# A graph network's bf16 splits: casts moved from VectorE and GpSimd to ScalarE, and the graph layers' output rows in two halves of PSUM

## The reference, cut to what matters

```python
# mean layers (run twice):  MEAN1, MEAN2
mean = segment_sum(h[src], dst) / max(count, 1);  out = mean @ W_l + b_l + h @ W_r
# graph convolutions (three): GCN1, GCN2, GCN3
h = x @ W
out = segment_sum(h[src] * dis[src] * dis[dst], dst) + h * dis**2 + b
# around each layer: x = layernorm(x + layer(x))
```

## Time and profile before

| what | value |
|---|---|
| median of 3 runs | 8144.81 us (8144.05 to 8150.12) |
| profiled execution, its own time | 8149.13 us |
| its span in the profile | 8147.2 us |
| busy shares | PE 52%, DVE 62%, ACT 35%, POOL 59% |

### The profile page before, as it was taken

The page is one execution under the profiler, slowest core; times in us unless marked ns, Lnnn a source line. Parts: engine busy times, 40 slices in busy tenths (PEclk is TensorE's granted clock), DMA queues, the critical chain, the costliest instruction groups (busy, mean ns, idle before and its releaser), DMA issues.

```text
span 8147.2 us, 70764 instructions
## 1 busy us (share of the span) xinstructions
PE 4234.8 (52%) x19184; PEld 2471.1 (30%) x19184; DVE 5020.9 (62%) x9411; ACT 2884.7 (35%) x5375; POOL 4827.2 (59%) x5030
## 2 busy tenths in 40 slices
PE   2110000000255555666665566566566598999999
PEld 1000000000131111111113111111111398999999
DVE  4654444444568888888786778878887774222232
ACT  0222222222255555555553555555555300010000
POOL 6777777777637777777776777777777500000000
PEclk6555555555565555555555555555555599999999
DMA  5333333333224444444443444444444275766767
GB/s 132 88 98 85 85 87 87 85 85 85 66 86 131 130 131 133 132 131 133 133 131 101 133 131 131 133 133 131 131 133 132 84 268 199 267 223 220 267 228 248
DMA packets 642166, 1129.68 MB, mean 139 GB/s; under 512 B 164844, under 2 KB 422271, under 8 KB 641618
## 3 DMA queue, kind: packets, MB, share of 16 engines
q1 hardware_dynamic: 360112, 437.17, 17.2%
q0 software_dynamic: 159184, 251.10, 14.8%
q10 hardware_dynamic: 122578, 438.40, 13.6%
HBM read 713.46 MB, written 412.70 MB: 138 GB/s over the span
## 4 chain that ended last, share of the span: by engine, by line
POOL 48%; PE 21%; issue 17%; DVE 10%; DMA 4%; ACT 1%; DVEq 0%; POOLq 0%; SPq 0%; ACTq 0%
POOL CG L460 46%; PE psX L736 6%; PE psB L736 6%; PE psA L736 6%; DMA CG<-table,BUF 3%; DVE BUF L1550 2%; PE psO L679 1%; DVE XTQ L1576 1%; DVE BUF L1545 1%; DVE STG L1576 1%; DVE BUF L1542 1%; DVE XTQ L1569 1%; DVE STG L1569 1%; ACT X L1045 1%; POOL EG L519 1%
## 5 line engine op out<-in xcount | busy, mean ns | idle before, releaser
L460 POOL DMA_INDIRECT CG<-table,BUF x4704 | 4482.0, 953 | 1567.5 <-issue 1351.7
L706 PE MATMUL psO<-WE,BUF 128*128 128x384 f32 x1568 | 1141.7, 883 | 381.7 <-DMA BUF<-in_edge_attr 381.7
L1001 ACT ACTIVATE BUF<-iota,EG 128x128 bf16<-128x128 f16 x3136 | 958.0, 387 | 205.1 <-ACT CG L981 103.0
L779 PE MATMUL psA<-ident,F 128*100 128x128 f32 x1 | 0.5, 455 | 1704.3 <-DVEq L1451 1704.3
L486 POOL CAST CG<-EG x35 | 26.9, 769 | 1296.1 <-DVEq L1217 1296.1
L977 ACT COPY psX<-BUF 128x384 f32<-128x384 f32 x392 | 189.0, 482 | 1540.0 <-DVE XTQ L1576 771.0
L706 PEld LDWEIGHTS psO<-WE,BUF 128*128 128x128 f32 x1568 | 459.6, 323 | 893.8 <-DMA BUF<-in_edge_attr 646.5
L1542 DVE TENSOR_SCALAR BUF<-iota,EG 128x392 bf16<-128x392 f16 x1568 | 562.1, 358 | 46.9 <-DMA EG<-step_rows 19.1
L1480 DVE TENSOR_TENSOR terms<-CG,ARENA 128x64 f32<-128x64 f32 x98 | 26.3, 269 | 904.2 <-DMA CG<-table,BUF 903.7
L1545 DVE TENSOR_SCALAR BUF<-iota,EG 128x392 bf16<-128x392 f16 x1568 | 543.4, 347 | 6.5 <-PE psB L716 3.3
L779 PEld LDWEIGHTS psA<-ident,F 128*100 128x100 f32 x1 | 0.2, 162 | 1704.7 <-DVEq L1451 1704.7
(11 more groups left out here) (284 smaller groups left out, 7533.6 us busy)
## 6 DMA issues: line engine op xcount, KB each, us to landing
BUF<-counts SPq DMA_DIRECT2D x245, 784.0 KB, 5.8
BUF<-counts ACTq DMA_DIRECT2D x245, 784.0 KB, 6.4
counts<-BUF SPq DMA_DIRECT2D x1572, 98.0 KB, 2.3
hist<-CG ACTq DMA_DIRECT2D x392, 384.0 KB, 2.4
hist<-CG ACTq DMA_DIRECT2D x196, 416.0 KB, 2.5
CG<-table,BUF POOLq DMA_INDIRECT x4704, 2.5
BUF<-in_edge_attr SPq DMA_DIRECT2D x392, 128.0 KB, 3.3
table<-TB SPq DMA_DIRECT2D x14, 336.0 KB, 2.6
```

Of the source, the lines that this page charges most:

```text
L460: pool.indirect_dma_start(out=rows_in[:, u % RING, k, :], out_offset=None, in_=tab, in_offset=bass.IndirectOffsetOnAxis(ap=SRC[:, u * S + ...
L706: mm = pe.matmul(ETERM[:, s, a, 0:4 * DIM], EA[:, s, a, :], WE[:, m, :, :].rearrange("k c d -> k (c d)"), start=True, stop=True)
L1001: far = nc.scalar.activation(FAR[:, j, a, :], iota16[:, 0:P], ACT.Square, bias=STEP[:, 2 + a, u * CS + j:u * CS + j + 1], scale=-1.0)
```

## The change

It touches only the node rows of MEAN2, GCN1, GCN2 and GCN3 (`SPLIT_HERE`); MEAN1 stays as it was. There:

- ACT casts both parts (new functions `first_part` and `second_part`); DVE does both subtractions (`rest_of_first`, `third_part`), the third part of group g-1 between the table of group g and the rest of group g. GpSimd's loops over these four phases go; only its loop for MEAN1 stays.
- In the three graph phases the product of group g goes to half g % 2 of psO, and PE waits for the table of group g-2 instead of g-1.
- In code order on ACT, the last casts stand behind the last copy of XT (or R) and ahead of the loading loop.

```diff
@@ PE, multiply_group
-                pe.wait_ge(out_used, g + (base + 1))
+                narrow = f in (GCN1, GCN2, GCN3)
+                pe.wait_ge(out_used, base + (max(g, 1) if narrow else g + 1))
@@ ACT, node_phase
                 rows_transposed(f, g)
                 if g and f in (MAX1, MAX2, MEAN1, MEAN2):
                     root_rows(f, g - 1)
+                if g and f in SPLIT_HERE:
+                    if g >= 2:
+                        second_part(f, g - 2)
+                    first_part(f, g - 1)
             if f in (MAX1, MAX2, MEAN1, MEAN2):
                 root_rows(f, NG - 1)
+            if f in SPLIT_HERE:
+                second_part(f, NG - 2)
+                first_part(f, NG - 1)
+                second_part(f, NG - 1)
+
+        def first_part(f, g):
+            act.wait_ge(table_made, PASS_OF_PHASE[f] * NG + g + 1)
+            nc.scalar.copy(PARTS[:, here, 0:DIM], TBW[:, here, :]).then_inc(first_made, 1)
+
+        def second_part(f, g):
+            act.wait_ge(rest_made, (PASS_OF_PHASE[f] - GATHER_PASSES) * NG + g + 1)
+            nc.scalar.copy(PARTS[:, here, DIM:2 * DIM], EGW[:, here, :]).then_inc(second_made, 1)
@@ DVE, take_rows
-                split(here, g)
+                if f in SPLIT_HERE:
+                    if g:
+                        third_part(f, g - 1)
+                    rest_of_first(f, g)
+                else:
+                    split(here, g)
+
+        def rest_of_first(f, g):
+            dve.wait_ge(first_made, SPLIT_HERE.index(f) * NG + g + 1)
+            link(tt(EGW[:, here, :], TBW[:, here, :], PARTS[:, here, 0:DIM], ALU.subtract))
+            dve.sem_inc(rest_made, 1)
+
+        def third_part(f, g):
+            dve.wait_ge(second_made, (PASS_OF_PHASE[f] - GATHER_PASSES) * NG + g + 1)
+            tt(PARTS[:, here, 2 * DIM:3 * DIM], EGW[:, here, :], PARTS[:, here, DIM:2 * DIM],
+               ALU.subtract).then_inc(parts_made, 1)
```

More of the change, by code:

```diff
@@ L72 @@
 MAX_PASSES = (1, 2)
+SPLIT_HERE = (MEAN2, GCN1, GCN2, GCN3)
 EARLY, LATE = slice(0, NB - GB), slice(NB - GB, NB)
@@ L282, in build @@
     OUTG = psO[:, 0:GB * OUT_COLS].rearrange("p (j c) -> p j c", c=OUT_COLS)
+    OUT2 = psO[:, :].rearrange("p (s j c) -> p s j c", s=2, c=P)
     ETERM = psO[:, :].rearrange("p (s b c) -> p s b c", s=2, b=2)
@@ L356, in build @@
     large_known = sem("large_known")
+    first_made = sem("first_made")
     rest_made = sem("rest_made")
@@ L523, in _ @@
         second_and_third_parts(0)
-        for n in range(1, 8 - GATHER_PASSES):
-            second_and_third_parts(n)
     @block.sync
@@ L676, in multiply_group @@
                 pe.wait_ge(xt_copied, f * NG + g + 1)
-                pe.wait_ge(out_used, g + (base + 1))
+                narrow = f in (GCN1, GCN2, GCN3)
+                pe.wait_ge(out_used, base + (max(g, 1) if narrow else g + 1))
                 for k in range(GB):
-                    mm = pe.matmul(OUTG[:, k, 0:cols], XT[0:depth, g % 2, k * P:(k + 1) * P], WR[0:depth, f, 0:cols],
+                    mm = pe.matmul(OUT2[:, g % 2, k, 0:cols] if narrow else OUTG[:, k, 0:cols], XT[0:depth, g % 2, k * P:(k + 1) * P], WR[0:depth, f, 0:cols],
                                    start=True, stop=f != PROJ)
@@ L912, in node_phase @@
                     root_rows(f, g - 1)
+                if g and f in SPLIT_HERE:
+                    if g >= 2:
+                        second_part(f, g - 2)
+                    first_part(f, g - 1)
             if f in (MAX1, MAX2, MEAN1, MEAN2):
                 root_rows(f, NG - 1)
+            if f in SPLIT_HERE:
[3 more added lines that the diff above has]
+        def first_part(f, g):
+            here = slice(g * GB, (g + 1) * GB)
+            act.wait_ge(table_made, PASS_OF_PHASE[f] * NG + g + 1)
+            nc.scalar.copy(PARTS[:, here, 0:DIM], TBW[:, here, :]).then_inc(first_made, 1)
+        def second_part(f, g):
+            here = slice(g * GB, (g + 1) * GB)
+            act.wait_ge(rest_made, (PASS_OF_PHASE[f] - GATHER_PASSES) * NG + g + 1)
+            nc.scalar.copy(PARTS[:, here, DIM:2 * DIM], EGW[:, here, :]).then_inc(second_made, 1)
         def attention_pass():
@@ L1243, in take_rows @@
                 if f in (GCN1, GCN2, GCN3):
-                    tt(TBW[:, here, :], OUTG[:, :, 0:DIM], dis[:, here].unsqueeze(2).broadcast_to([P, GB, DIM]),
+                    tt(TBW[:, here, :], OUT2[:, g % 2, 0:GB, 0:DIM], dis[:, here].unsqueeze(2).broadcast_to([P, GB, DIM]),
                        ALU.mult).then_inc(table_made, 1)
@@ L1258, in node_rows @@
                 take_rows(f, g)
+            if f in SPLIT_HERE:
+                third_part(f, NG - 1)
+                dve.wait_ge(parts_made, (PASS_OF_PHASE[f] - GATHER_PASSES + 1) * NG)
             rows_taken(f)
```

## The result

The changed kernel took 8168.82 us (median of 11 runs, 8162.36 to 8176.47), the kernel before beside it 8148.51 (8143.21 to 8152.92): a ratio of 1.0025, 95% interval 1.0017 to 1.0033. It is 20.3 us slower, where 21.7 were forecast. The profiled execution has a span of 8172.0 us, 24.8 more than before; 2.6 of them were there when MEAN1's last products began (6501.67 against 6499.12), ahead of anything that the change touches.

A forecast was written before the change was run, and what follows sets the result against it. PE's blocks run at 6.00 us each, so only the stretch to each phase's second block could move: 6.3 + 6.1 + 6.1 + 3.2 = +21.7 us on 8144.8 gave 8166.5 us, 8 in 10 between 8155 and 8181.

The forecast's parts named there:

- ACT's DMAs behind the casts: Ends of node rows: ACT's halves of blocks 0 to 2 start after the last cast, delaying the second block; +21.7 us summed.
- The chain's first term: End of node rows on ACT: from the start of the last ACT instruction to its DMA, 1.1 us.
- The second: Start of a phase's sum: from ACT's DMA issue to PE's second block, 12.25 us.
- MEAN2: MEAN2's first block, already held by ACT's DMA: everything put ahead of that DMA counts in full, +3.2 us.
- The graph phases: GCN1, GCN2 and GCN3: the second block starts later by 6.3, 6.1 and 6.1 us.
- the start of the table of group 2: DVE in graph phases: starts when it did, at 7169.52, 7499.69 and 7824.24, with 2.90 us a group from there.
- GpSimd's part in the 1.56: DVE's rest in graph phases: 1.56 us beside GpSimd's third part, 0.86 without; group 0.69 us less, at 2.90.
- The casts: Two casts on ACT at 0.8 us each: ACT does 2.5 us a graph-phase group, under DVE's 2.90.
- That rival: Casts on ACT at 1.37 us make ACT the bound in graph phases and lengthen MEAN2's groups: 8185 us, chance 0.07.
- The two halves: psO in graph phases: the second half only lets PE keep ahead of DVE; worth nothing by itself.
- The rival that the transfer doesn't hold the block: First blocks: parts set the second block; -4.3, -4.6, -4.6 in graph phases, nothing in MEAN2; 8131 us, chance 0.10.
- The clock rival: Graph phases' first blocks: after longer PE idle, whole block at 0.50 takes 12 us, four more each; 8179, chance 0.05.

The follow-up runs named there:

- experiment 1: Changed kernel, but SP starts both halves of the first three blocks of MEAN2, GCN1, GCN2 and GCN3: 8130.09 us, ratio 0.9974 to the kernel before.
- experiment 3: Kernel before, split untouched, with one added wait: ACT's loading loop waits for the phase's last rest: 8182.27 us, ratio 1.0038.
- experiment 4: Changed kernel with psO as one buffer again: 8173.72 us, ratio 1.0028 to the kernel before.
- experiment 7: Experiment 1 with psO as one buffer, run twice in slow rounds: 9263.57 and 9292.89 us, ratios 0.9981 and 0.9974 to the kernel before.
- experiment 2: Kernel before, with SP starting both halves of the first three blocks in the four phases, nothing else: 8146.81 us, ratio 0.9994.

## Why the prediction was right, and where a term was off

**ACT's DMAs behind the casts.** Right, and shown from both sides: experiment 1 takes the DMAs away and leaves the casts, and the loss turns into a gain; experiment 3 brings the wait alone, and the loss is there. The chain's first term held: last cast to DMA 1.0 to 1.2 us (1.1 taken). The second held in two phases of four: DMA to second block 12.24 in MEAN2 and 12.35 in GCN1, but 13.66 in GCN2 and 13.49 in GCN3 (12.25 taken).

**MEAN2.** +3.2 forecast, +3.2 measured. The rows of that phase kept their pace (tables 4.31 us apart), since ACT's casts fit between R and XT.

**The graph phases.** +6.3, +6.1, +6.1 forecast, +5.9, +9.6, +3.5 measured. The sum, 18.5 and 19.0, agrees; the pieces do not, and that they cancel is luck. What was mis-sized is the start of the table of group 2, taken as in the trace before: counted from the second block of the phase before, it came 0.1 us later in GCN1, 2.0 later in GCN2 and 3.1 sooner in GCN3. The granted clock goes with it. In GCN2 PE was at 0.50 for longer, to about 7515.8, 14 us after its first product (7501.38), where before it had been 6 us, and the table of group 2 came 3.53 us ahead of that of group 3; in GCN3 it was at 1.00 from the first transposes, and the first table came 2.0 us sooner. Windows of the changed kernel, GCN2 and then GCN3:

```profile
7512.00:7514.00 2.00, 2.00 (x11) 0.50 0.01 4
7514.00:7516.00 2.00, 2.00 (x13) 0.55 0.00 0
...
7834.00:7836.00 2.00, 1.57 (x15) 1.00 0.39 159
```

The longer way from DMA to second block in these two phases is 1.4 and 1.2 us more. Against it the groups from there on were 0.5 us shorter in all than the sum had them in GCN1 and GCN3. What decides which phase gets the fast start is not shown by any run here.

**GpSimd's part in the 1.56.** Right: with GpSimd silent the subtractions take 0.85 and 0.86. In experiment 3, with GpSimd at its parts again, the rest takes 1.55. The group is 2.78, not 2.90.

**The casts.** 0.75 us, the value that the L1005 row gave, where 0.8 was taken and 1.37 was the upper bound. That rival is out.

**The two halves.** "Worth nothing by itself" was right for this change (experiment 4: 0.6 us) and wrong as a statement on the edit: once the loads are in time it is worth 10.8 us (experiment 7), of which the shorter group explains 1 to 2.

**The rival that the transfer doesn't hold the block.** Out as a forecast. Its price can be held against experiment 1, where the transfer no longer holds the block. It gave -13.5 in the graph phases, which came out at -11.5, and "nothing in MEAN2", but MEAN2's block had been held by the same transfer, and freeing it brought 7.6 us more.

**The clock rival** (a whole first block at 0.50, 12 us) did not come as priced; after idles of almost 10 us the first blocks took 7.8 to 9.1, so two of them (9.10 and 8.73) were 1.0 to 1.4 us over the 7.7 of the sum.

## What to carry to other kernels

An engine that computes and also starts transfers has one stream: what is put ahead of a transfer delays it, even when it fills time in which the engine was idle. Before giving such an engine work, look at what stands behind that work, and start the transfer as soon as its buffer is free, on that engine or another. Here the same split is 20 us slower or 21 faster than the kernel before, depending on where three DMA starts a phase stand. Of the 21, some 8 come from MEAN2's load, which the kernel before could have had without the split (experiment 2), though it gave half of that back elsewhere. And a second buffer that shortens a group by only 0.09 us was worth 11 us in three phases, once the loads were early.

## What the runs showed that was not expected

- In experiment 7 the clock fell in an idle of 1.1 us between two products and stayed at 1.2 GHz for some 6.8 us: 1.5 us more for the products and some 2 from the last table to the second block (GCN1, in both traces alike). In GCN1 of experiment 4 it stayed at 2.4 GHz through the same idle.
- Sizes of single stages moved with the clock by up to 4 us a phase (GCN2 +9.6, GCN3 +3.5) while their sum came out as forecast. A single stage of one trace is a poor measure of such an edit; the sum over phases is better, and even that differs by up to 3 us between two executions of one kernel.
- In some rounds every kernel took 13 to 14% longer, the kernel before too. In the trace that was compared above, 1100 us of that lie in GpSimd's gathers, busy and idle together, while the last sum kept its time to 0.1 us in all traces.
